# Six damage items of an attention step made by a GpSimd negation and an accumulating DMA, ten kept on VectorE

## The chip, the core and the metric

The kernel runs on one core of a Trainium2 chip. The metric is the device time of one launch in microseconds, the median of several runs. Engines are named as in the profile: PE is TensorE, DVE is VectorE, ACT is ScalarE, POOL is GpSimd, SP is SyncE, which here only issues DMAs.

## What is computed

One transformer layer over x of shape (8, 1024, 128), fp32: a layer norm, then windowed attention and a routed feed-forward (160 experts, 8 chosen for each token) side by side. The change touches the attention alone. With 16 heads and a window of 64 positions, cut to what matters:

```python
disp_win = _windows(disp, 64)                    # (B, heads, T, 64, 16)
strain = disp_win - disp[:, :, :, None, :]
bond_act = gelu(strain @ W_strain + rel_emb @ W_pos)
bond_logits = (bond_act @ W_bond)[..., 0]
damage_act = gelu(strain @ W_dmg + b_dmg)
damage = sigmoid((damage_act @ W_dmg_out)[..., 0] + b_dmg_out[0])
logits = bond_logits - 10.0 * damage
weights = softmax(where(cmask, logits, -inf))
out = einsum('bntd,bntde->bnte', weights, val_win)
```

The products with W_strain and W_dmg are linear in the displacements, so the kernel projects every token once. What is left for a token and a window position is a difference of two projected values, then the gelu.

## The kernel before

The program has five stages: constants, projections and router, `attend(c, 0)`, the experts, `attend(c, 1)`. The two calls of `attend` cover half of the batch each. One call walks over 8 chunks of 512 tokens, each in two steps, one for each group of 8 heads (`par` 0 and 1): 16 steps for each call, 32 in all. Step s has 16 items, n = 0 to 15. Item n is a tile of 128 partitions (8 heads by 16 channels) by 8 window positions by 512 tokens, 4096 fp32 values in a partition, 2 MB in all. Even n are bond items (`ty` 0), odd n are damage items (`ty` 1). An item goes through three engines:

1. The difference of the shifted window (`s_win[..., d0+1 : ...]`) and the values at the token itself ("here"). On DVE "here" comes from PSUM (`ps_here`, which PE fills at L1181). A bond item without bias on ACT is 8 SCALAR_TENSOR_TENSOR (L1102), which add the position term `rpos` as well; a damage item, and in the second call the bond items 6 and 14 (`BIASED`), is one TENSOR_TENSOR of 4096 (L1097). On POOL (L947) it is one TENSOR_TENSOR of two operands in SBUF. `POOL_ITEMS = (3,)`: the damage items 3, 7, 11 and 15 are POOL's, the twelve others DVE's.
2. ACT: one gelu in place (L1001 damage, L1003 bond; 8 for a biased item, L997).
3. PE: matmuls that sum the channels into `ps_l` (L1198), then `item_done`.

DVE has three item buffers: item n waits until item n - 4 is through PE. POOL has two (`u_pool`): item n waits for item n - 8.

Each engine has its own copy of the order, written out by hand, and takes the items strictly in order with other work in between. ACT: tanh (L1010), copies for the softmax (L1019, items 5 to 8), copies of transposed weights (L1032, items 9 to 15 and 0), exp (L1024, item 12, with two table loads). DVE: logits (L1120), mask, maximum, subtraction (L1131, L1135, L1138, items 8 to 11), the sum, its reciprocal and in the first call the multiply by it (L1142, L1145, L1148, item 15); in the second call also 32 additions of routed rows (L1074), 8 at each of the items 0, 4, 8 and 12. POOL: behind each of the items 3, 7, 11 and 15 `route`, 8 indirect DMAs (L926 scatters rows in the first call, L935 gathers them in the second); at item 3 of every second step `spread` (L913), which waits until PE has finished the value products of the chunk before (`av_done`, the last of them at PE's item 1 of the same step); at item 5 of the same steps an addition (L959); at item 15 of the second call the multiply by the reciprocal (L963), which waits for DVE's L1145.

SP loads the windows (L765), waiting in L757 to L763 until every subtraction that reads the same `s_win` is through, and carries the weights to DRAM and back (L793, L799, 2 MB back for each step).

Of the kernel before, what the change touches and what calls it, by code (L numbers as in the profile page):

```python
# [32 lines left out]
TOPK = 8  # L33
POOL_ITEMS = (3,)
BIASED = (6, 14)


def moe_attention_layer(nc, x, w_dispT, w_val, relT, w_strain, w_pos, w_bond, w_dmg, b_dmg,
# [28 lines left out]
    with ExitStack() as ctx:  # L67
# [3 lines left out]
        def sem(name):  # L71
            return ctx.enter_context(nc.semaphore(name))
# [38 lines left out]
        def sb(name, shape, dt=F32, c=ctx):  # L111
            return c.enter_context(nc.sbuf_tensor(name, shape, dt))
# [542 lines left out]
        win_loaded = [sem(f"win_loaded{g}") for g in range(HG)]  # L655
        sub_dve, sub_pool, gelu_done, item_done = sem("sub_dve"), sem("sub_pool"), sem("gelu_done"), sem("item_done")
        tanh_done, logits_in = sem("tanh_done"), sem("logits_in")
# [15 lines left out]
        def attend(c, half):  # L673
# [7 lines left out]
            chunk0 = (1 - half) * NCH // 2 - it0  # L681
            u_dve = sb(f"u_dve_{half}", [P, 3, 8, TC], F32, c)
            u_pool = sb(f"u_pool_{half}", [P, 2, 8, TC], F32, c)
            s_win = sb(f"s_win_{half}", [P, HG, 2, SW], F32, c)
# [24 lines left out]
            ps_u = c.enter_context(nc.psum_tensor(f"ps_u_{half}", [P, TC], F32))  # L709
            on_pool = POOL_ITEMS  # L710
            NP = len(on_pool)
            dve_of = [sum(q % 4 not in on_pool for q in range(n + 1)) for n in range(NI)]
            pool_of = [n + 1 - dve_of[n] for n in range(NI)]
            ND, NPI = dve_of[-1], pool_of[-1]

# [23 lines left out]

            def item_buffer(n):  # L740

                if n % 4 in on_pool:
                    return u_pool[:, (pool_of[n] - 1) % 2]
                return u_dve[:, (n % 4 - sum(q < n % 4 for q in on_pool))]

            def buffer_free(n):

                if n % 4 in on_pool:
                    return n + 1 - 8 // NP
                return n - 3  # L750

            with nc.Block() as block:
                @block.sync
                def _(sp):
                    def load_windows(b, tc, it, par):

                        if some(it):  # L757
                            if some(ND * (2 * it + par - 1)):
                                sp.wait_ge(sub_dve, ND * (2 * it + par - 1))
                                sp.sem_inc(held, 1)  # L760
                            if some(NPI * (2 * it + par - 1)):
                                sp.wait_ge(sub_pool, NPI * (2 * it + par - 1))
# [134 lines left out]
                def _(pool):  # L897
# [41 lines left out]
                    def step(s, it, par, st):  # L939
                        for n in range(NI):  # L940
                            cgrp, d0, ty = offsets(n)
                            if "i" in st and n % 4 in on_pool:
                                if pool_of[n] == 1:
                                    pool.wait_ge(win_loaded[par], 32 * it + 32)
                                if some(NI * s + buffer_free(n)):
                                    pool.wait_ge(item_done, NI * s + buffer_free(n))
# [27 lines left out]
                def _(act):  # L974
# [7 lines left out]
                    def step(s, it, par, st):  # L982
                        for n in range(NI):
# [3 lines left out]
                            if "i" in st:  # L987
                                if n % 4 in on_pool:
                                    if some(NPI * s + pool_of[n]):
                                        act.wait_ge(sub_pool, NPI * s + pool_of[n])  # L990
                                else:
                                    if some(ND * s + dve_of[n]):
                                        act.wait_ge(sub_dve, ND * s + dve_of[n])
                                u = item_buffer(n)
# [54 lines left out]
                def _(dve):  # L1049
# [28 lines left out]
                    def step(s, it, par, st):  # L1078
                        for n in range(NI):
# [5 lines left out]
                            if sums and "i" not in st:  # L1085
                                for d in range(8):
                                    add_routed(s - first, 1 - par, 2 * n + d)
                            if "i" in st and n % 4 not in on_pool:
                                if dve_of[n] == 1:
                                    dve.wait_ge(win_loaded[par], 32 * it + 32)  # L1090
                                    dve.wait_ge(here_done, s + 1)

                                if some(NI * s + buffer_free(n)):
                                    dve.wait_ge(item_done, NI * s + buffer_free(n))
                                here = ps_here[:, ty, :]
                                if ty or n in biased:
                                    last = dve.tensor_tensor(item_buffer(n), windows(par, ty, d0, 8),  # L1097
                                                             here.unsqueeze(1).to_broadcast([P, 8, TC]), ALU.subtract)
                                else:

                                    for d in range(8):
                                        last = dve.scalar_tensor_tensor(  # L1102
                                            out=item_buffer(n)[:, d, :], in0=s_win[:, par, ty, d0 + d + 1:d0 + d + 1 + TC],
                                            scalar=rpos[:, d0 + d:d0 + d + 1], in1=here, op0=ALU.add, op1=ALU.subtract)
# [49 lines left out]
                def _(pe):  # L1154
# [30 lines left out]
                    def step(s, it, par, st):  # L1185
                        more = "i" in st and (not isinstance(s, int) or s + 1 < end)
                        for n in range(NI):
                            cgrp, d0, ty = offsets(n)
                            if "i" in st:
# [6 lines left out]
                                for d in range(8):  # L1196
                                    q, g = (d0 + d) % 16 // 4, d % 4
                                    last = pe.matmul(ps_l[32 * g:32 * g + 32, cgrp % 2, ty, :], wsel[:, ty, q, :],  # L1198
                                                     item_buffer(n)[:, d, :], start=(q == 0), stop=(q == 3))
                                last.then_inc(item_done, 1)  # L1200
# [264 lines left out]
```

## Time and profile before

| | |
|---|---|
| median of 3 runs | 4021.71 us (4020.48 to 4023.9) |
| the profiled execution | 4033.82 us, span 4032.3 us |
| busy, share of the span | DVE 84%, ACT 64%, PE 63%, POOL 61% |
| first call of attend, from 379 us to 1722 us | DVE 1318.45 us busy of 1342.70 |
| experts, 1722 us to 2371 us | not touched |
| second call, 2371 us to 4032 us | DVE 1540.48 us busy of 1661.00 |

Times are read from one execution. A group's line gives busy time, the mean of one instruction and, behind the bar, the idle time of its engine just before the instructions and what ended it. PE's busy time is pipelined, so it says little of its limit.

### The profile page before, as it was taken

Reading aid. Unit: us, or ns where it says so; the run is one execution under the profiler, and the core shown is the slowest. Engines: PE = TensorE matmul, PEld = TensorE weight load, DVE = VectorE, ACT = ScalarE, POOL = GpSimd, SP = SyncE. Lnnn points to the kernel's source line nnn. Section 1 sums busy time; section 2 is a strip of 40 time slices with the busy share of each in tenths; the row PEclk is TensorE's granted clock in tenths of the full one; section 3 lists DMA queues with packets and bytes.
Section 4 is the critical chain, followed back from the end, with each engine's and each line's share of the span. In section 5 each row is a group of like instructions: output and inputs, shape, how many; then the busy total and the mean of one; then the engine's idle time right before and its main releaser. Section 6 shows DMA issues by size and latency. Waiting matters only on the chain. (4 is left out here: it accounts for less than half of the span.)

```text
span 4032.3 us, 64337 instructions
## 1 busy us (share of the span) xinstructions
PE 2547.4 (63%) x20970; PEld 1282.8 (32%) x20970; DVE 3379.6 (84%) x4350; ACT 2576.9 (64%) x1812; POOL 2476.6 (61%) x1748
## 2 busy tenths in 40 slices
PE   5661556766666666668888864565666656565556
PEld 3440112322222222246667631122222222222224
DVE  6886999999999999923433369999999999999993
ACT  1111878888788887833333356777777777777773
POOL 1222887668787787813333467677767767676762
PEclk9885878888888888879999987777878787878886
DMA  7883121322222222127887841222222222222222
GB/s 258 304 304 99 37 74 63 96 81 78 72 70 84 91 80 75 58 79 235 243 243 240 244 139 32 68 65 74 64 75 64 75 64 75 64 75 64 74 63 81
DMA packets 376227, 445.81 MB, mean 111 GB/s; under 512 B 49185, under 2 KB 291697, under 8 KB 376050
## 3 DMA queue, kind: packets, MB, share of 16 engines
q1 hardware_dynamic: 293106, 283.77, 22.4%
q0 software_dynamic: 58752, 148.46, 11.3%
q10 hardware_dynamic: 24192, 11.02, 1.0%
q8 instruction: 134, 2.20, 0.2%
q14 instruction: 43, 0.35, 0.0%
HBM read 239.08 MB, written 204.02 MB: 110 GB/s over the span
## 5 line engine op out<-in xcount | busy, mean ns | idle before, releaser
L1198 PE MATMUL ps_l<-u_dve,wsel 128*32 128x512 f32 x6144 | 1004.0, 780 | 1001.8 <-ACT u_dve L1003 640.7
L1102 DVE SCALAR_TENSOR_TENSOR u_dve<-s_win,rpos,ps_here 128x512 f32<-128x512 f32 x1792 | 1225.8, 737 | 74.3 <-PE ps_here L1181 51.4
L1003 ACT ACTIVATE u_dve<-u_dve 128x4096 f32<-128x4096 f32 x224 | 809.9, 3616 | 427.8 <-DVE u_dve L1102 427.0
L947 POOL TENSOR_TENSOR u_pool<-s_win 128x4096 f32<-128x4096 f32 x128 | 1021.9, 7983 | 9.7 <-PE ps_l L1198 6.9
L1097 DVE TENSOR_TENSOR u_dve<-s_win,ps_here 128x4096 f32<-128x4096 f32 x160 | 703.0, 4409 | 0.0
L1198 PEld LDWEIGHTS ps_l<-u_dve,wsel 128*32 128x32 f32 x6144 | 211.1, 128 | 1447.7 <-issue 647.1
L926 POOL DMA_INDIRECT xslot_dram<-xr,slot_now x512 | 520.0, 1016 | 154.1 <-issue 147.8
L935 POOL DMA_INDIRECT yg<-yslot_dram,slot_now x512 | 499.1, 975 | 164.6 <-issue 144.1
L1001 ACT ACTIVATE u_dve<-u_dve,bdmg_sb 128x4096 f32<-128x4096 f32 x128 | 474.6, 3708 | 91.5 <-DVE u_dve L1097 86.8
L1001 ACT ACTIVATE u_pool<-u_pool,bdmg_sb 128x4096 f32<-128x4096 f32 x128 | 473.7, 3701 | 27.7 <-POOL u_pool L947 27.5
L1391 DVE TENSOR_TENSOR hs<-sg,ps_e 128x512 f32<-128x512 f32 x168 | 115.4, 687 | 382.6 <-ACT sg L1376 382.6
L1074 DVE SCALAR_TENSOR_TENSOR acc<-yg,gate_now,acc 128x128 f32<-128x128 f32 x512 | 358.9, 701 | 1.0
L1198 PE MATMUL ps_l<-u_pool,wsel 128*32 128x512 f32 x2048 | 267.2, 636 | 113.9 <-ACT u_pool L1001 113.3
L1168 PE MATMUL ps_o<-at_sb,v_msk 128*32 128x64 f32 x4096 | 303.7, 235 | 0.1
L1168 PEld LDWEIGHTS ps_o<-at_sb,v_msk 128*32 128x32 f32 x4096 | 268.7, 120 | 75.0 <-issue 56.0
L1369 ACT ACTIVATE xsT<-ps_x 128x512 f32<-128x512 f32 x168 | 100.3, 597 | 277.8 <-PE ps_x L1329 277.8
L1032 ACT ACTIVATE at_sb<-ps_u 128x512 f32<-128x512 f32 x256 | 150.8, 589 | 190.9 <-PE ps_o L1168 162.1
L963 POOL TENSOR_TENSOR ml<-ml,winv 128x2048 f32<-128x2048 f32 x16 | 72.6, 4537 | 320.2 <-DVE slot_now L1058 184.2
L1407 POOL DMA_DIRECT2D yslot_dram<-ys x168 | 128.1, 762 | 216.4 <-DVE ys L1397 189.3
L1246 PEld LDWEIGHTS ps_u<-ident,band 128*128 128x128 f32 x1024 | 148.2, 198 | 297.3 <-issue 183.5
L1246 PE MATMUL ps_u<-ident,band 128*128 128x128 f32 x1024 | 203.7, 329 | 58.1 <-ACT at_sb L1032 39.4
L1138 DVE TENSOR_TENSOR ml<-ml,mx 128x512 f32<-128x512 f32 x128 | 205.4, 1604 | 4.4
(142 smaller groups left out, 3366.2 us busy)
## 6 DMA issues: line engine op xcount, KB each, us to landing
band<-band_dram SPq DMA_DIRECT2D x32, 2048.0 KB
xslot_dram<-zero SPq DMA_DIRECT2D x16, 2688.0 KB, 10.1
xs<-xslot_dram SPq DMA_DIRECT2D x168, 256.0 KB, 3.6
yslot_dram<-ys POOLq DMA_DIRECT2D x168, 256.0 KB, 3.2
band_dram<-ml SPq DMA_DIRECT2D x64, 512.0 KB
we<-in_w_expert SPq DMA_DIRECT2D x336, 64.0 KB, 2.8
s_win<-s_dram SPq DMA_DIRECT2D x64, 288.0 KB, 8.2
s_dram<-s_sb POOLq DMA_DIRECT2D x16, 1024.0 KB, 4.6
```

What stands on the lines that cost most here:

```text
L926: pool.indirect_dma_start(xslot_dram, bass.IndirectOffsetOnAxis(ap=slot_now[:, par, i:i + 1], axis=0), xr[:, par, j, :], None).then_inc(sc ...
L935: pool.indirect_dma_start(yg[:, i, :], None, yslot_dram, bass.IndirectOffsetOnAxis(ap=slot_now[:, par, i:i + 1], axis=0)).then_inc(gathere ...
L947: pool.tensor_tensor(item_buffer(n), windows(par, ty, d0, 8), s_win[:, par, ty, PAD:PAD + TC].unsqueeze(1).to_broadcast([P, 8, TC]), ALU.s ...
L1001: act.activation(u, u, ACT.Gelu, bias=bdmg_sb[:]).then_inc(gelu_done, 1)
L1003: act.activation(u, u, ACT.Gelu).then_inc(gelu_done, 1)
L1074: dve.scalar_tensor_tensor(out=acc[:, old, j, :], in0=yg[:, i, :], scalar=gate_now[:, old, i:i + 1], in1=acc[:, old, j, :], op0=ALU.mult, ...
L1097: last = dve.tensor_tensor(item_buffer(n), windows(par, ty, d0, 8), here.unsqueeze(1).to_broadcast([P, 8, TC]), ALU.subtract)
L1102: last = dve.scalar_tensor_tensor(out=item_buffer(n)[:, d, :], in0=s_win[:, par, ty, d0 + d + 1:d0 + d + 1 + TC], scalar=rpos[:, d0 + d:d0 ...
L1138: dve.tensor_tensor(ml[:, j], ml[:, j], mx[:, j, :].unsqueeze(1).to_broadcast([P, D, HH]), ALU.subtract).then_inc(centred, 1)
L1168: last = pe.matmul(ps_o[32 * g:32 * g + 32, j * P + half * HALF:j * P + (half + 1) * HALF], v_msk[:, 2 * j + half, 32 * h:32 * h + 32], at ...
L1198: last = pe.matmul(ps_l[32 * g:32 * g + 32, cgrp % 2, ty, :], wsel[:, ty, q, :], item_buffer(n)[:, d, :], start=(q == 0), stop=(q == 3))
L1246: last = pe.transpose(ps_u[:, i * P:(i + 1) * P], band[:, k // 2, 4 * (k % 2) + i:BANDW:HH], ident[:])
```

## The change

Six damage items of a step, 3, 5, 7, 11, 13 and 15, are made in two parts. POOL writes the negated "here" values, broadcast over the 8 positions, into the item's buffer with one TENSOR_SCALAR (multiply by -1), waits for its own semaphore, and issues an accumulating DMA that adds the 8 shifted windows from `s_win` onto that buffer, SBUF to SBUF. ACT waits for the DMA's semaphore (one for each buffer) in place of POOL's. The damage items 1 and 9 and all bond items are DVE's, ten in all. The numbers of buffers stay 3 and 2, but both sets now rotate over the items of their own kind: a DMA item waits for the second last DMA item before it, a DVE item for the third last DVE item. SP's load of the windows waits for `gelu_done` of the earlier step's items in place of the two subtraction semaphores. The cut diff:

```diff
-POOL_ITEMS = (3,)
+DMA_ITEMS = (3, 5, 7, 11, 13, 15)
+DVE_BUFS = 3
+DMA_BUFS = 2
...
+            def slot_of(m):
+                par, n = m // NI % 2, m % NI
+                if n in DMA_ITEMS:
+                    return "dma", (par * NM + DMA_ITEMS.index(n)) % DMA_BUFS
+                return "dve", (par * ND + on_dve.index(n)) % DVE_BUFS
...
+            def buffer_free(par, n):
+                m = par * NI + n
+                back = next(k for k in range(1, 2 * NI + 1) if slot_of(m - k) == slot_of(m))
+                return n - back + 1
...
-                            if some(ND * (2 * it + par - 1)):
-                                sp.wait_ge(sub_dve, ND * (2 * it + par - 1))
...
+                            if some(NI * (2 * it + par - 1)):
+                                sp.wait_ge(gelu_done, NI * (2 * it + par - 1))
...
-                                pool.tensor_tensor(
-                                    item_buffer(n), windows(par, ty, d0, 8),
-                                    s_win[:, par, ty, PAD:PAD + TC].unsqueeze(1).to_broadcast([P, 8, TC]),
-                                    ALU.subtract).then_inc(sub_pool, 1)
+                                u = item_buffer(par, n)
+                                pool.tensor_scalar(
+                                    u, s_win[:, par, ty, PAD:PAD + TC].unsqueeze(1).to_broadcast([P, 8, TC]),
+                                    -1.0, None, ALU.mult).then_inc(base_set, 1)
+                                pool.wait_ge(base_set, NM * s + k + 1)
+                                pool.sem_inc(held, 1)
+                                pool.dma_start(u, windows(par, ty, d0, 8), accum_op=ALU.add)\
+                                    .then_inc(sub_dma[landed(it, par, n)[0]], 16)
...
-                                if n % 4 in on_pool:
-                                    if some(NPI * s + pool_of[n]):
-                                        act.wait_ge(sub_pool, NPI * s + pool_of[n])
+                                if n in DMA_ITEMS:
+                                    i, count = landed(it, par, n)
+                                    act.wait_ge(sub_dma[i], count)
...
-                            if "i" in st and n % 4 not in on_pool:
+                            if "i" in st and n not in DMA_ITEMS:
```

## Rows read from the trace of the kernel before

**Rows 1.** Windows over 11 steps of each call: busy us (x instructions), granted clock, DMA
```profile
core 0: us, PE busy (x) PEld busy (x) DVE busy (x) ACT busy (x) POOL busy (x), PEclk, DMA share, GB/s
706.40:1644.50 938.10, 619.84 (x4860) 261.11 (x4852) 923.66 (x936) 782.78 (x398) 719.38 (x445) 0.88 0.25 79
2746.00:3844.00 1098.00, 665.62 (x4852) 267.14 (x4848) 1064.18 (x1123) 816.05 (x563) 766.42 (x461) 0.80 0.23 70
```
**Rows 2.** Groups of DVE in the first call's window, 706.4:1644.5
```profile
L1102 DVE SCALAR_TENSOR_TENSOR u_dve<-s_win,rpos,ps_here 128x512 f32<-128x512 f32 x704 | 468.8, 737 | 11.8 <-PE ps_here L1181 11.8
L1097 DVE TENSOR_TENSOR u_dve<-s_win,ps_here 128x4096 f32<-128x4096 f32 x44 | 194.0, 4410 | 0.0
...
L1142 DVE TENSOR_REDUCE wsum<-ml 128x32 f32<-128x2048 f32 x11 | 42.7, 3879 | 0.0
```
**Rows 3.** Groups of ACT and POOL in the first call's window
```profile
L1003 ACT ACTIVATE u_dve<-u_dve 128x4096 f32<-128x4096 f32 x89 | 321.8, 3616 | 81.5 <-DVE u_dve L1102 81.1
...
L1001 ACT ACTIVATE u_pool<-u_pool,bdmg_sb 128x4096 f32<-128x4096 f32 x44 | 162.9, 3702 | 23.2 <-POOL u_pool L947 23.2
L1032 ACT ACTIVATE at_sb<-ps_u 128x512 f32<-128x512 f32 x88 | 51.8, 589 | 41.6 <-PE ps_o L1168 41.5
...
L1024 ACT ACTIVATE ml<-ml 128x2048 f32<-128x2048 f32 x11 | 21.0, 1911 | 0.1
L1024 ACT ACT_TABLE_LOAD x11 | 14.1, 1283 | 0.2
...
L926 POOL DMA_INDIRECT xslot_dram<-xr,slot_now x348 | 358.1, 1029 | 99.9 <-issue 99.9
L947 POOL TENSOR_TENSOR u_pool<-s_win 128x4096 f32<-128x4096 f32 x43 | 343.2, 7981 | 0.8
L913 POOL COPY v_msk<-v_raw 128x128 f32<-128x128 f32 x48 | 11.6, 293 | 123.6 <-PE ps_o L1168 104.1 <-issue 19.5
```
**Rows 4.** Group of POOL in the second call's window, 2746:3844
```profile
L963 POOL TENSOR_TENSOR ml<-ml,winv 128x2048 f32<-128x2048 f32 x11 | 49.9, 4540 | 221.4 <-DVE slot_now L1058 120.8 <-DVE winv L1145 100.6
```
**Rows 5.** Groups of POOL over the whole span
```profile
L1407 POOL DMA_DIRECT2D yslot_dram<-ys x168 | 128.1, 762 | 216.4 <-DVE ys L1397 189.3 <-issue 27.0
L1306 POOL DMA_DIRECT2D we<-in_w_expert x168 | 90.1, 536 | 121.4 <-issue 67.7 <-PE ps_z L1355 53.1 <-DVE ys L1397 0.7
...
L898 POOL MEMSET v_msk<- 128x4096 f32 x2 | 7.0, 3508 | 73.4 <-POOLq L620 68.8 <-POOLq L1278 4.7
```
**Rows 6.** Timeline of one hand-over from ACT to PE, first call
```profile
902.75 3.61 ACT L1003 ACTIVATE u_dve<-u_dve 128x4096 f32<-128x4096 f32 x1
...
906.41 1.92 PE L1198 MATMUL ps_l<-u_dve,wsel 128*32 128x512 f32 x16 [0.50 <-ACT u_dve L1003]
```
**Rows 7.** DMA issues: KB each, us to landing
```profile
s_dram<-s_sb POOLq DMA_DIRECT2D x16, 1024.0 KB, 4.6
...
band_dram<-zero SPq DMA_DIRECT2D x1, 4096.0 KB, 12.4
```
**Rows 8.** DVE lines with two operands in SBUF: ns min/median/max, whole span
```profile
L1074 DVE SCALAR_TENSOR_TENSOR acc<-yg,gate_now,acc x512: 258/339/8114, 2444.0 to 3970.5; 128x128 f32<-128x128 f32 x171
L1138 DVE TENSOR_TENSOR ml<-ml,mx x128: 691/693/8456, 488.9 to 3967.2; 128x512 f32<-128x512 f32 x128
```
**Rows 9.** Timeline: one DVE addition, then a POOL subtraction and a DVE subtraction beside it
```profile
3116.75 7.80 DVE L1074 SCALAR_TENSOR_TENSOR acc<-yg,gate_now,acc 128x128 f32<-128x128 f32 x1
...
929.20 8.20 POOL L947 TENSOR_TENSOR u_pool<-s_win 128x4096 f32<-128x4096 f32 x1
...
933.40 4.55 DVE L1138 TENSOR_TENSOR ml<-ml,mx 128x512 f32<-128x512 f32 x1
```
**Rows 10.** Waits of SP, the window loads' own
```profile
SPq L760 <- DVE u_dve L1102: 60.9, 1, 60.9
SPq L760 <- DVE u_dve L1097: 59.9, 1, 59.9
```

More of the change, by code:

```diff
@@ L655, in moe_attention_layer @@
         win_loaded = [sem(f"win_loaded{g}") for g in range(HG)]
-        sub_dve, sub_pool, gelu_done, item_done = sem("sub_dve"), sem("sub_pool"), sem("gelu_done"), sem("item_done")
+        sub_dve, gelu_done, item_done = sem("sub_dve"), sem("gelu_done"), sem("item_done")
+        base_set, sub_dma = sem("base_set"), [sem(f"sub_dma{i}") for i in range(DMA_BUFS)]
         tanh_done, logits_in = sem("tanh_done"), sem("logits_in")
@@ L681, in attend @@
             chunk0 = (1 - half) * NCH // 2 - it0
-            u_dve = sb(f"u_dve_{half}", [P, 3, 8, TC], F32, c)
-            u_pool = sb(f"u_pool_{half}", [P, 2, 8, TC], F32, c)
+            u_dve = sb(f"u_dve_{half}", [P, DVE_BUFS, 8, TC], F32, c)
+            u_dma = sb(f"u_dma_{half}", [P, DMA_BUFS, 8, TC], F32, c)
             s_win = sb(f"s_win_{half}", [P, HG, 2, SW], F32, c)
@@ L709, in attend @@
             ps_u = c.enter_context(nc.psum_tensor(f"ps_u_{half}", [P, TC], F32))
[L710 to L714, printed above, removed]
+            on_dve = [n for n in range(NI) if n not in DMA_ITEMS]
+            dve_of = [sum(q in on_dve for q in range(n + 1)) for n in range(NI)]
+            ND, NM = len(on_dve), len(DMA_ITEMS)
+            def slot_of(m):
[3 more added lines that the diff above has]
+                return "dve", (par * ND + on_dve.index(n)) % DVE_BUFS
             def steps(e, step):
@@ L738, in windows, with item_buffer, landed @@
                 return bass.AP(row.tensor, row.offset, [list(row.ap[0]), [1, nd], [1, TC]])
-            def item_buffer(n):
-                if n % 4 in on_pool:
[L743 to L750, printed above, removed]
+            def item_buffer(par, n):
+                which, i = slot_of(par * NI + n)
+                return (u_dma if which == "dma" else u_dve)[:, i]
+            def buffer_free(par, n):
+                m = par * NI + n
+                back = next(k for k in range(1, 2 * NI + 1) if slot_of(m - k) == slot_of(m))
+                return n - back + 1
+            def landed(it, par, n):
+                i = slot_of(par * NI + n)[1]
+                uses = [m for m in range(2 * NI) if slot_of(m) == ("dma", i)]
+                return i, 16 * (len(uses) * it + sum(m <= par * NI + n for m in uses))
             with nc.Block() as block:
@@ L987, in step @@
                             if "i" in st:
[L988 to L994 removed]
+                                if n in DMA_ITEMS:
+                                    i, count = landed(it, par, n)
+                                    act.wait_ge(sub_dma[i], count)
+                                else:
+                                    act.wait_ge(sub_dve, ND * s + dve_of[n])
+                                u = item_buffer(par, n)
                                 if n in biased:
@@ L1091, in step @@
                                     dve.wait_ge(here_done, s + 1)
-                                if some(NI * s + buffer_free(n)):
-                                    dve.wait_ge(item_done, NI * s + buffer_free(n))
+                                if some(NI * s + buffer_free(par, n)):
+                                    dve.wait_ge(item_done, NI * s + buffer_free(par, n))
                                 here = ps_here[:, ty, :]
                                 if ty or n in biased:
-                                    last = dve.tensor_tensor(item_buffer(n), windows(par, ty, d0, 8),
+                                    last = dve.tensor_tensor(item_buffer(par, n), windows(par, ty, d0, 8),
                                                              here.unsqueeze(1).to_broadcast([P, 8, TC]), ALU.subtract)
@@ L1102, in step @@
                                         last = dve.scalar_tensor_tensor(
-                                            out=item_buffer(n)[:, d, :], in0=s_win[:, par, ty, d0 + d + 1:d0 + d + 1 + TC],
+                                            out=item_buffer(par, n)[:, d, :], in0=s_win[:, par, ty, d0 + d + 1:d0 + d + 1 + TC],
                                             scalar=rpos[:, d0 + d:d0 + d + 1], in1=here, op0=ALU.add, op1=ALU.subtract)
@@ L1198, in step @@
                                     last = pe.matmul(ps_l[32 * g:32 * g + 32, cgrp % 2, ty, :], wsel[:, ty, q, :],
-                                                     item_buffer(n)[:, d, :], start=(q == 0), stop=(q == 3))
+                                                     item_buffer(par, n)[:, d, :], start=(q == 0), stop=(q == 3))
                                 last.then_inc(item_done, 1)
```

13 lines of the change are left out of this document (6 added, 7 removed).

## The prediction

> **What bounds the kernel now.** I read the windows first. Over 11 steps of the first call DVE is busy 923.7 of 938.1 us, that is 84.0 of 85.3 us a step; ACT 71.2 and POOL 65.4. Over 11 steps of the second call a step is 99.8 us, with DVE at 96.7, ACT at 74.2, POOL at 69.7 [rows 1]. The groups of DVE come next: its large ones wait for nobody but 11.8 us for PE [rows 2], while ACT waits for DVE (81.1 us before the bond gelus) [rows 3]. So DVE sets the pace in both calls. DMA is busy 25% and 23% [rows 1]. POOL looks idle a quarter of the time, but its busy time leaves out the issue gaps: 8 scatters a group cost (358.1 + 99.9) / 348 = 1.32 us each, 10 us after each of four items, 40 us a step [rows 3]. POOL really has 32 us of subtractions and 42 us of other work in an 85 us step.
>
> **What leaves.** DVE loses items 5 and 13 and keeps 1 and 9: two TENSOR_TENSOR of 4.41 us, 8.8 us a step [rows 2]. POOL loses four subtractions of 7.98 us, 31.9 us [rows 3]. If DVE stayed the bound, that would be 32 x 8.8 = 282 us.
>
> **A POOL item.** The trace has no one-operand POOL instruction of this size. A memset of the same 4096 columns takes 3.51 us and reads nothing; the two-operand subtraction takes 7.98 [rows 5, 3]. Those are the bounds; I take 4.0, near the memset, since only one operand is added. The issue: 64 KB take 0.54 us and 256 KB 0.76 [rows 5]; for 1024 rows of 2 KB I take 1.1, between 0.8 and 2. With 0.2 for its own semaphore an item costs POOL 5.3 us, six cost 32: nothing is saved there. The Trainium skill (GPSIMD Engine Reference, Engine selection) calls one-input work on GpSimd roughly line-rate; 4096 columns at the 1.2 GHz of its specifications are 3.4 us by that, an estimate, and every POOL item would be 0.6 us cheaper.
>
> **The transfer**, the largest unknown. Copies of 1024 and 4096 KB land after 4.6 and 12.4 us [rows 7]: 2.6 us a MB and 2.0 fixed. The accumulating one writes 2 MB but has two 2 MB inputs, windows and negation. Lower bound: the second input is free, 5.2 us of data. Upper: two reads and a write in series, 15.6. I take the two reads in series with the write beside them, 10.4. Six of these are 62 us a step beside the 20 that are there, out of 85, so they meet: with half of the present 25% share falling into them, 10.4 becomes 12. It then lands 12 + 2.0 - 1.1 = 13 us after its issue ends, and a second one behind it no sooner than 12 us after the first. The rule "the accumulate reads its destination and writes it later" (the Trainium skill, DMA: Bandwidth & Descriptors, Rules for kernel authors) speaks against the change in the same direction; no row here shows such a transfer.
>
> **The loop.** A DMA item goes round: negate and issue 5.3, land 13, gelu 3.7 [rows 3], PE 2.8 (it ends 2.0 us after the gelu in [rows 6], more at the lower clock). POOL waits for the buffer with all its queue behind it: item 7 for 3, 11 for 5, 13 for 7, 15 for 11, 3 for 13, 5 for 15. Due times in the first call, zero when item 3's issue ends; 15 of the step before was issued at -15.3 (a route group of 10 and item 3 lie between). Step with no `spread`: 3 is through ACT at 17.3 and PE at 20.1; POOL issues 5 at 15.3 and 7 at 25.4; they land at 28.3 and 40.3; 5 is through PE at 34.8; 7 leaves ACT at 44.0; 11 is issued at 40.7, but ACT has 8 to 11 and small copies, 17.1 us, so 11 leaves ACT at 61.1 and PE at 63.9; 15 is issued at 69.2; a route group, and item 3 of the next step (13 is through PE at 76.4) at **84.5**. Step with `spread`: PE's item 1 and the values are done at 13.1, copies to 15.1, so 5 is issued at 30.4, 7 at 37.0; they land at 43.4 and 55.4; 11 leaves ACT at 76.2; 15 at 84.3; next item 3 at **99.6**. `spread` costs POOL 17 us a time now as well (104.1 us before six groups of 8 copies [rows 3]), hidden because a POOL item has 8 items' time to come round; that cover goes. A pair takes 184.1 against 170.6 now: +13.5 x 8 = +108.
>
> Second call: after 15, POOL's multiply waits for DVE's reciprocal, and the route group and item 3 queue behind it. 11 leaves ACT at 61.1, 12 at 64.8, exp with its tables (1.9 + 2 x 1.28 [rows 3]) 69.3, DVE's sum 3.9 [rows 2] and reciprocal 73.6, multiply 4.5 [rows 4], route, item 3: **93.5**. With `spread`, 4 us of wait and 2.4 of copies, everything 6.4 later: **99.9**. A pair 193.4 against 199.6: -6.2 x 8 = -50. POOL's 20 us wait a step for the reciprocal (221.4 us in 11 [rows 4]) is about what the loop uses up.
>
> **At no cost.** The window load waits for a later event, but is needed a step on; SP waited for it only at the start, 60.9 and 59.9 us [rows 10]; cover gone, it would cost up to a step. Scatters and gathers queue behind the accumulates by up to 12 us, and are read a step later. DVE's three rotating buffers only reach further ahead. Contention: a DVE line with two SBUF operands stretches beside a POOL subtraction: 339 ns at the median and 8114 at most, 693 and 8456 [rows 8], and one took 4.55 us until the POOL instruction ended [rows 9]. The Trainium skill (SBUF — State Buffer, Who interferes with whom) says that such a DVE instruction contends with any GpSimd instruction that reads SBUF. By that the negation blocks too, 24 us a step against 32. It matters only if DVE binds; I count it at nothing.
>
> **Sum.** 4033.8 + 108 - 50 = 4092 for the profiled execution, which stands 12.1 above the median of the runs: **4080 us**, 1.4% slower. One us more or less on the transfer's data is felt twice a step, at the landings of 5 then 7 and at 11 or the sum: 2 x 32 = 64 us. Clean 10.4 us of data gives 4080 - 1.6 x 64 = 3978; the whole 25% share in the way, 13.9, gives 4202. That is this case's own range.
>
> **Rivals.** About 0.2%, 8 us, is what a measurement of this kernel can tell from no change.
>
> Rival 1, faster: the second input is nearly free and the transfer lands in 6 to 8 us. Then DVE's saving comes through until ACT or POOL binds: the first call's step cannot go under POOL's 74 plus part of `spread`, say 78, the second under DVE's 96.7 - 8.8 = 88. That gives 16 x (7.3 + 11.8) = 306 less, 3720 at best; 3800 if half the waits stay. For: copies of 4 MB run at 2.6 us a MB with 25% load. Against: two inputs. Chance 0.18.
>
> Rival 2, DMA becomes the bound: 15.6 us of data, six and the 20 now there are 114 us a step. Both calls then run at 114: 16 x (28.7 + 14.2) = +686, 4710. It decides from where the six pass 65 us in the first call. For: nothing in the trace shows the adder's rate. Chance 0.12.
>
> Rival 3, POOL's own work: negation at 6 us and issue at 2 make an item 8.2, three of them lie on the path of a step, +2.9 x 3 x 32 = +278, 4360. Chance 0.10.
>
> My forecast's case has 0.60: of it 0.20 ends faster by over 0.2%, where the interference is small, 0.07 within, 0.33 slower. Together: faster 0.38, same 0.07, slower 0.55. Range 3820 to 4300: it takes the own range, most of rival 1 and the near part of 3, and leaves out about 0.1 on either side.
>
> **What would show it.** The duration of the POOL TENSOR_SCALAR (4.0), the accumulate's issue (1.1) and landing (14 from its start); ACT's wait before damage gelus passing from POOL and DVE to a DMA; POOL's waits for PE before the negations; DVE's busy share falling to about 0.85 in the first call with waits for PE. Right steps would show 84 and 100 us in turn in the first call. Wrong it is if a landing takes under 10 us, if DVE still runs at 98%, or if DMA is busy over 95%.

## The result and the profile after

| | before | changed |
|---|---|---|
| median of 4 runs | 4021.43 us | 5278.18 us (5270.16 to 5282.32) |
| span of the profiled execution | 4032.3 us | 5280.8 us |
| DVE, ACT, POOL busy, share of the span | 84%, 64%, 61% | 69%, 49%, 72% |

The changed kernel is slower by a factor of 1.313 (95% interval 1.311 to 1.315), 1257 us. The forecast was 4080 us, 59 slower, with a range from 3820 to 4300: the direction was right, the size was not, by a factor of twenty. The first view is the table of windows over the same 11 steps of each call as in [rows 1]; the columns are those of [rows 1].

```profile
core 0: us, PE busy (x) PEld busy (x) DVE busy (x) ACT busy (x) POOL busy (x), PEclk, DMA share, GB/s
851.50:2300.10 1448.60, 674.03 (x4844) 276.98 (x4844) 878.77 (x914) 781.88 (x397) 1183.05 (x538) 0.73 0.73 147
3577.00:5050.50 1473.50, 703.94 (x4844) 276.17 (x4844) 1290.71 (x1101) 817.95 (x562) 1234.80 (x550) 0.73 0.74 147
```

A step of the first call went from 85.3 to 131.7 us, one of the second from 99.8 to 134.0. Times 16 each that is 742 and 547, together a little over the whole loss, since the first steps of each call lost less. DVE no longer sets the pace in the first call: 79.9 us busy a step. POOL is busy 107.5. PE's granted clock read 0.88 before and reads 0.73 now in the first call, where PE is busy 47% of the time in place of 66%.

Next, the groups of POOL in the first of these windows; [rows 3] has their counterparts.

```profile
L963 POOL TENSOR_SCALAR u_dma<-s_win 128x4096 f32<-128x4096 f32 x66 | 710.5, 10766 | 12.2 <-PE ps_l L1216 10.8
L939 POOL DMA_INDIRECT xslot_dram<-xr,slot_now x352 | 354.1, 1006 | 106.3 <-issue 105.7 <-PE ps_l L1216 0.6
L968 POOL DMA_DIRECT2D u_dma<-s_win x66 | 111.0, 1681 | 47.1 <-POOL u_dma L963 28.4 <-issue 12.1 <-DVE slot_now L1076 6.6
...
L926 POOL COPY v_msk<-v_raw 128x128 f32<-128x128 f32 x48 | 11.6, 287 | 99.9 <-PE ps_o L1186 87.2 <-issue 12.7
```

The one-operand multiply takes 10.77 us, more than the two-operand subtraction that it replaces (7.98 [rows 3]). The issue takes 1.68. With the wait between them (28.4 + 12.1 + 6.6 over 66) an item holds POOL for 13.2 us, six hold it for 79, the routing for 42 more: 121 of the 131.7 us. Nearly all of the rest is the value copies and the stand before them, (99.9 + 11.6) / 11 = 10.1 us. POOL waits for an item's buffer 10.8 us in 11 steps. The buffer loop, on which the forecast's due times rest, is not where the time goes: POOL reaches each item so late that its buffer has long been free. The timeline of POOL shows one stand (start, duration, instruction, idle before it):

```profile
1131.36 1.71 POOL L968 DMA_DIRECT2D u_dma<-s_win  x1 [0.61 <-POOL u_dma L963]
1151.30 1.94 POOL L926 COPY v_msk<-v_raw 128x128 f32<-128x128 f32 x8 [18.24 <-PE ps_o L1186]
```

The steps of the first call alternate accordingly, mostly 122 and 142 us. POOL's waits in the second call's window (us in total, times, longest) show the same queue there:

```profile
POOL yg L948 <- issue: 104.0, 348, 0.3
POOL u_dma L968 <- POOL u_dma L963: 44.9, 65, 1.0
POOL ml L982 <- DVE winv L1163: 37.2, 3, 13.6
POOL v_msk L926 <- PE ps_o L1186: 31.9, 3, 10.9
POOL ml L982 <- DVE slot_now L1076: 13.6, 1, 13.6
```

A step has 112.3 us of POOL's busy time and 13.5 of gaps at its own issues; it stands 4.6 for DVE's reciprocal and 2.9 before the value copies. That is 133.3 of 134.0 us: POOL's queue fills the step in both calls.

Two views answer to the transfer: the issues by line (KB each, us to landing), and the DMA queue of POOL (packets, MB, share of 16 engines), 11.3% before.

```profile
u_dma<-s_win POOLq DMA_DIRECT2D x192, 2048.0 KB, 15.1
...
q0 software_dynamic: 258432, 551.13, 54.0%
```

If the rest of this queue costs what it did before (456 us; it is 456 and 460 in two later runs without the transfers), 192 transfers took 0.540 x 5280.8 - 0.113 x 4032.3 = 2396 us of all 16 engines, 12.5 us each. A transfer lands 15.1 us after its start at the median and 14.1 at the least.

### The profile page after: what moved, and what is told of

It reads as the page before. It is cut to its first block and busy times, and to the rows that moved or that the text cites. A ratio compares the mean times of both kernels' runs of the same rounds, so it can differ in the third digit from the quotient of the medians.

```text
span 5280.8 us, 64909 instructions
## 1 busy us (share of the span) xinstructions
PE 2683.3 (51%) x20970; PEld 1305.1 (25%) x20970; DVE 3630.5 (69%) x4286; ACT 2580.1 (49%) x1812; POOL 3814.6 (72%) x2004
## 5 line engine op out<-in xcount | busy, mean ns | idle before, releaser
L963 POOL TENSOR_SCALAR u_dma<-s_win 128x4096 f32<-128x4096 f32 x192 | 2068.8, 10775 | 25.3 <-PE ps_l L1216 20.9
L1216 PE MATMUL ps_l<-u_dma,wsel 128*32 128x512 f32 x3072 | 647.7, 988 | 1605.1 <-ACT u_dma L1019 1605.1
L1019 ACT ACTIVATE u_dma<-u_dma,bdmg_sb 128x4096 f32<-128x4096 f32 x192 | 711.8, 3707 | 1359.7 <-DMA u_dma<-s_win 1359.6
L1216 PE MATMUL ps_l<-u_dve,wsel 128*32 128x512 f32 x5120 | 757.5, 708 | 614.4 <-ACT u_dve L1021 410.9
L1092 DVE SCALAR_TENSOR_TENSOR acc<-yg,gate_now,acc 128x128 f32<-128x128 f32 x512 | 677.2, 1323 | 1.9 <-DMA acc<-part_dram 0.9
L1216 PEld LDWEIGHTS ps_l<-u_dma,wsel 128*32 128x32 f32 x3072 | 113.0, 152 | 1917.5 <-ACT u_dma L1019 1389.2
L1115 DVE TENSOR_TENSOR u_dve<-s_win,ps_here 128x4096 f32<-128x4096 f32 x96 | 423.4, 4410 | 0.0
L968 POOL DMA_DIRECT2D u_dma<-s_win x192 | 322.6, 1680 | 133.7 <-POOL u_dma L963 105.4
L1156 DVE TENSOR_TENSOR ml<-ml,mx 128x512 f32<-128x512 f32 x128 | 341.4, 2667 | 4.4
L1186 PEld LDWEIGHTS ps_o<-at_sb,v_msk 128*32 128x32 f32 x4096 | 271.6, 121 | 79.9 <-issue 61.7
L1019 ACT ACTIVATE u_dve<-u_dve,bdmg_sb 128x4096 f32<-128x4096 f32 x64 | 237.0, 3703 | 45.6 <-DVE u_dve L1115 45.6
## 6 DMA issues: line engine op xcount, KB each, us to landing
u_dma<-s_win POOLq DMA_DIRECT2D x192, 2048.0 KB, 15.1
```

Of the source, the lines that this page charges most:

```text
L963: pool.tensor_scalar(u, s_win[:, par, ty, PAD:PAD + TC].unsqueeze(1).to_broadcast([P, 8, TC]), -1.0, None, ALU.mult).then_inc(base_set, 1)
L968: pool.dma_start(u, windows(par, ty, d0, 8), accum_op=ALU.add)\
L1092: dve.scalar_tensor_tensor(out=acc[:, old, j, :], in0=yg[:, i, :], scalar=gate_now[:, old, i:i + 1], in1=acc[:, old, j, :], op0=ALU.mult, ...
L1115: last = dve.tensor_tensor(item_buffer(par, n), windows(par, ty, d0, 8), here.unsqueeze(1).to_broadcast([P, 8, TC]), ALU.subtract)
L1156: dve.tensor_tensor(ml[:, j], ml[:, j], mx[:, j, :].unsqueeze(1).to_broadcast([P, D, HH]), ALU.subtract).then_inc(centred, 1)
L1186: last = pe.matmul(ps_o[32 * g:32 * g + 32, j * P + half * HALF:j * P + (half + 1) * HALF], v_msk[:, 2 * j + half, 32 * h:32 * h + 32], at ...
```

## The experiments

The theory after this reading: POOL's queue is the bound, and the multiply overfills it. The rivals: the transfers bound it, a hidden wait of the loop, or contention between POOL and DVE. Where no ratio is given, a kernel has one time; the kernel before beside them stood between 4011 and 4028 us.

### The multiply, replaced in three ways

```diff
-                                pool.tensor_scalar(
-                                    u, s_win[:, par, ty, PAD:PAD + TC].unsqueeze(1).to_broadcast([P, 8, TC]),
-                                    -1.0, None, ALU.mult).then_inc(base_set, 1)
+                                pool.memset(u, 0.0).then_inc(base_set, 1)
```

> The negation is replaced by a memset of the same 4096 columns, so the damage items leave out the token's own value. Theory (POOL's queue is the bound, and the negation of 10.6 us is what overfills it): the memset takes 3.5 us, a POOL item 6.1 us, POOL's work of a step falls from 120 to 78 us, and the buffer loop of the prediction decides: with 15 us landings about 88 us a step without the value copies and 103 with them, 4200 us in all. Rival (the accumulating transfer itself is the bound, with DMA 73% busy): the time stays above 4700 us and DMA's busy share rises over 0.9.

```diff
+                                pool.tensor_copy(
+                                    u, s_win[:, par, ty, PAD:PAD + TC].unsqueeze(1).to_broadcast([P, 8, TC]))\
+                                    .then_inc(base_set, 1)
```

> The negation is replaced by a copy of the same broadcast row (the minus sign is left out). Theory A (any one-operand POOL instruction over 4096 columns with a broadcast input is slow): the copy takes about 10 us and the time stays at 5280 us. Theory B (the multiply by a constant is slow, the pattern is not): the copy takes 4 to 5 us and the time falls to 4250 us or so.

```diff
+                                pool.tensor_tensor(
+                                    u, zero[:, 0:TC].unsqueeze(1).to_broadcast([P, 8, TC]),
+                                    s_win[:, par, ty, PAD:PAD + TC].unsqueeze(1).to_broadcast([P, 8, TC]),
+                                    ALU.subtract).then_inc(base_set, 1)
```

> The negation is written as a two-operand subtraction, a broadcast row of zeros minus the broadcast row; the result is the same as the changed kernel's. Theory (the one-operand form is dearer than the two-operand one): the subtraction takes 8.2 us as in the kernel before, a POOL item 10.8 us, a step 106 us and with the value copies 126: about 4800 us. Rival (writing beside an accumulating transfer slows any POOL instruction, so the subtraction stretches too): it takes over 10 us and the time stays near 5280.

Measured: 4338 us with the memset, 4345 with the copy, 5067 with zeros minus the row. The groups of POOL and DVE over the whole span, the memset first:

```profile
L963 POOL MEMSET u_dma<- 128x4096 f32 x192 | 682.6, 3555 | 366.0 <-PE ps_l L1214 362.7 <-issue 2.5 <-DMA s_win<-s_dram 0.6
...
L1090 DVE SCALAR_TENSOR_TENSOR acc<-yg,gate_now,acc 128x128 f32<-128x128 f32 x512 | 180.8, 353 | 12.4 <-issue 11.4
```

the copy:

```profile
L963 POOL COPY u_dma<-s_win 128x4096 f32<-128x4096 f32 x192 | 701.0, 3651 | 357.8 <-PE ps_l L1216 353.6 <-issue 3.2 <-DMA s_win<-s_dram 0.5
...
L1092 DVE SCALAR_TENSOR_TENSOR acc<-yg,gate_now,acc 128x128 f32<-128x128 f32 x512 | 388.9, 759 | 9.0 <-issue 8.0
```

and the subtraction from zeros:

```profile
L963 POOL TENSOR_TENSOR u_dma<-zero,s_win 128x4096 f32<-128x4096 f32 x192 | 1732.7, 9024 | 31.2 <-PE ps_l L1217 27.9 <-DMA s_win<-s_dram 0.8
```

The same broadcast row is copied in 3.65 us and multiplied in 10.77. So the multiply is dear and the pattern is not: theory B of the copy's expectation. With seven us less an item, 933 us are gone (940 with the memset), and only now POOL waits for the buffers, 354 us. The rival of the memset run fell in its number (it wanted over 4700) but not in its mark: DMA's share rose to 0.94 in the first call. The time was 140 above my 4200. The zeros-minus form was expected at 8.2 us and 4800 us; it took 9.0 and 5067, between the theory and the rival (over 10 us, near 5280). The steps of its first call fell to 113 and 132 us in turn, those of its second only to 129 from 134, which the expectation had not seen. Why this subtraction takes 9.0 and not the 8.0 of the kernel before is open.

A finding beside it: DVE's additions with two SBUF operands take 353 ns at the mean with the memset, which only writes, 759 with the copy, which reads for 3.65 us, and 1323 in the changed kernel, where the multiply reads for 10.77. The last beside that of the kernel before:

```profile
L1074 DVE SCALAR_TENSOR_TENSOR acc<-yg,gate_now,acc 128x128 f32<-128x128 f32 x512 | 358.9, 701 | 1.0
...
L1092 DVE SCALAR_TENSOR_TENSOR acc<-yg,gate_now,acc 128x128 f32<-128x128 f32 x512 | 677.2, 1323 | 1.9 <-DMA acc<-part_dram 0.9
```

That the time hardly differs between memset and copy, 4338 and 4345, also says that this contention does not bound these two kernels. The three means agree with the Trainium skill (SBUF — State Buffer, Who interferes with whom), which sets writing apart from reading.

### The value copies at item 7

```diff
-                            if "a" in st and n == 3 and par == 0:
+                            if "a" in st and n == 7 and par == 0:
                                 spread(it - 1)
```

> The value copies of POOL (spread) move from item 3 to item 7 in its order, nothing else. Theory: in every second step POOL stands 18 us at item 3 for PE's value products, with the whole queue behind it; at item 7 they are long done, so every second step falls from 142 to about 124 us: 15 x 18 = 270 us less, about 5010 us. Rival (the wait only moves to another place, as POOL would otherwise wait for item buffers): under 100 us less.

Measured 5180 us, 98 less, against 270 expected: inside the rival's mark of under 100. The stand is gone, and the long steps of the first call fell from 142 to 127 us. The expectation took 18 us for all 15 copies; the changed kernel's whole wait there is 119.1 us for PE and 33.4 without a named releaser, 152 us, most of it in the first call.

### The negated row made elsewhere

The same result without the long multiply: ACT writes one negated row of 512 columns a step, POOL copies it over the positions; the value copies at item 7.

```diff
+                    def negate(s, it, par):
+                        if some(NM * s):
+                            act.wait_ge(base_set, NM * s)
+                        act.wait_ge(win_loaded[par], 32 * it + 32)
+                        act.activation(negrow[:], s_win[:, par, 1, PAD:PAD + TC], ACT.Copy, scale=-1.0).then_inc(neg_set, 1)
...
+                                pool.tensor_copy(
+                                    u, negrow[:].unsqueeze(1).to_broadcast([P, 8, TC])).then_inc(base_set, 1)
```

> ACT writes one negated row of 512 for the damage items once a step (0.6 us), POOL copies it over the 8 positions (3.6 us in place of 10.6), and the value copies stand at item 7: the same result with POOL's item at 6.2 us and no 18 us stand. Theory (with POOL relieved the two-buffer loop of the prediction is the bound, and half of what the value copies' wait cost comes off): 4345 us of the run with the copy alone, less about 8 x 18 in the first call and some 50 in the second: 4150 us, still slower than before. Rival (the loop's other waits refill it): 4300 or more.

Measured 4310 us: the rival. DMA was 94% busy in both calls. The same edit with four items, and the value copies back at item 3:

```diff
-DMA_ITEMS = (3, 5, 7, 11, 13, 15)
+DMA_ITEMS = (3, 7, 11, 15)
```

> The same negated row and copy, but only the four items 3, 7, 11 and 15 go through the accumulating DMA, as POOL's four did before; DVE has its twelve items again. POOL's item costs 6.2 us in place of 8.2, and of these only 3.6 us read SBUF beside DVE, so DVE's lines with two SBUF operands are held up for 14 us a step in place of 32. Theory (contention is worth half of DVE's 11 us of stretching): both calls 5 us a step shorter than in the kernel before, 3860 us. Rival (the longer way of an item, 27 us against 8, makes ACT wait): 4030 to 4150.

Measured 4079 us, a ratio of 1.016 (1.014 to 1.019), against 3860 expected: the rival again. POOL waited 246 us for ACT's row, a wait that the experiment itself brought in.

### Half a transfer, and four items with the multiply

The first edit stands on the kernel with the copy.

```diff
-                                pool.dma_start(u, windows(par, ty, d0, 8), accum_op=ALU.add)\
+                                pool.dma_start(u[:, 0:4], windows(par, ty, d0, 4), accum_op=ALU.add)\
```

> As the run with the copy, but the DMA adds only four of the eight windows (the other four are left out), so its data are 1 MB. Theory of the loop: 5.6 us less at each landing, felt twice a step, 32 x 11 = 358 us less than 4345, about 3990. Rival (POOL's queue of 78 us and the value copies are the bound, transfers are hidden): less than 100 us less.

Measured 3967 us, 379 below the run with the whole transfer. Once the multiply is gone, the transfer is on the path, 11.8 us a step for about half of its data. The number is near the expected 358, but not for the expectation's reason: DMA fell from 93% to 66% busy in the first call, and POOL's queue is what fills its steps of 88.1 us now, with 78.3 us of work and 8.2 of standing before the value copies; it waits for item buffers 1.4.

> The changed kernel with its own negation on POOL but only the items 3, 7, 11 and 15 by DMA. Theory (POOL's queue is the sum of its items at 13.2 us and 41 us of routing): 94 us a step, 112 with the value copies' wait, second call 94 to 110: about 4420 us. Rival (with six items DMA itself was the trouble, four are fine): under 4200.

The edit is that of the four items, on the changed kernel. Measured 4588 us, above both expectations. Its POOL group is 10.60 us an item, and the sum for POOL is right, 94 us and more. But the steps of the first call took 97 to 117 and those of the second 109 and 123 in turn. Over 11 steps of the first call, 106.4 us each, POOL's work is 95.3; the rest is the stand before the value copies, 7.9, and before the addition that waits for ACT, 3.1. In the second call, 116.8 us a step, POOL has 100.7 of work, 10.8 of waiting for DVE's reciprocal and 5.9 for ACT. So POOL's queue with its waits for others fills the step in both calls; the expectation had taken too little of the waits.

### Nobody waits for a row, four items

POOL negates one row of 512 columns itself once a step and copies it; the value copies at item 7, or at item 3.

```diff
+                                row = zero[:, par * TC:(par + 1) * TC]
+                                if k == 0:
+                                    pool.tensor_scalar(row, s_win[:, par, ty, PAD:PAD + TC], -1.0, None, ALU.mult)\
+                                        .then_inc(neg_set, 1)
+                                    pool.wait_ge(neg_set, s + 1)
+                                    pool.sem_inc(held, 1)
+                                pool.tensor_copy(u, row.unsqueeze(1).to_broadcast([P, 8, TC])).then_inc(base_set, 1)
```

> Four DMA items (3, 7, 11, 15); POOL negates one row of 512 columns itself once a step (1.4 us if the multiply costs 2.6 ns a column whatever its pattern) and copies it over the positions at each item, and the value copies stand at item 7. POOL then waits neither for ACT's row (246 us in the run with four items) nor 18 us for PE. Theory (with POOL on time the loop has slack, DVE is the bound with less contention): 83 us a step in the first call, 95 in the second, about 3900 us. Rival (POOL's lateness was harmless and the 15 us landing itself makes ACT late): 4040 to 4080 as before.

> As the run beside it, but the value copies stay at item 3. Theory: every second step of the first call stands up to 15 us on POOL, of which four items' distance hides part: 50 us more than the run beside it. Rival (hidden as in the kernel before): no difference.

Measured 3979 us (ratio 0.990, 0.989 to 0.992) and 3985 us (0.992, 0.991 to 0.994): both are faster than the kernel before, by one per cent and not the three expected, and by far faster than the changed one. The groups of POOL in the first of the two:

```profile
L969 POOL COPY u_dma<-zero 128x4096 f32<-128x4096 f32 x128 | 467.9, 3656 | 8.2 <-POOL zero L965 5.4 <-PE ps_l L1220 2.4
...
L965 POOL TENSOR_SCALAR zero<-s_win 128x512 f32<-128x512 f32 x32 | 49.1, 1534 | 24.5 <-PE ps_l L1220 16.2 <-issue 6.9 <-DMA s_win<-s_dram 0.7
```

512 columns, with no broadcast, cost 1.53 us, 3.0 ns a column; 4096 with a broadcast cost 2.6 a column. That is the second sign that the operation is slow whatever the pattern. In the eleven middle steps of each call this kernel stands at 85.8 and 99.6 us, as before. What it gains lies in the first four steps of each call, 309 us against 327 in the first and 353 against 375 in the second. DVE's additions fell from 701 to 505 ns, and in the first call DVE is busy only 79.0 us a step in place of 84.0. But it waits there for ACT's copies and exp (48 us in 11 steps) and for "here" from PE (19), and in the second call for item buffers on PE (82 us in 11 steps), waits that the kernel before has hardly or not at all. So most of what contention gave back went into waits; that the longer way of an item brings them is likely and not shown. The place of the value copies made no difference with four items.

### Without the transfer, and what bounds six items

```diff
-                                pool.wait_ge(base_set, NM * s + k + 1)
-                                pool.sem_inc(held, 1)
-                                pool.dma_start(u, windows(par, ty, d0, 8), accum_op=ALU.add)\
-                                    .then_inc(sub_dma[landed(it, par, n)[0]], 16)
...
-                                    i, count = landed(it, par, n)
-                                    act.wait_ge(sub_dma[i], count)
+                                    act.wait_ge(base_set, NM * s + DMA_ITEMS.index(n) + 1)
```

> The changed kernel without the accumulating DMA: ACT takes the negated value as it is, so the six items leave out the windows. Theory (POOL's queue alone sets the changed kernel's time): an item costs 10.9 us in place of 13.2, 14 us a step, 440 us less: 4840 us. Rival (the transfers carry a good part of the 1257 us): under 4600.

The other run is the edit of the section before (POOL's row, value copies at item 7) with all six items.

> Six DMA items as in the change, with POOL's own negated row once a step, the copies, and the value copies at item 7. Theory (with POOL at 80 us a step the transfers bound it: DMA was 94% busy in the run with ACT's row): 4250 to 4310, no better than that run's 4310. Rival (waiting for ACT's row cost it): 4150 or less.

Measured 4753 us without the transfer and 4318 for six items with POOL's row. The first is 526 below the changed kernel where POOL's shorter item alone explained 440, and still 737 above the kernel before, with no transfer in it at all: the multiply is enough to lose by. The multiply itself takes 10.59 us there, so the transfers beside it are not what makes it slow. Here are its windows:

```profile
780.00:1948.40 1168.40, 654.53 (x4844) 267.58 (x4844) 982.87 (x915) 783.41 (x398) 1065.50 (x473) 0.79 0.20 64
3162.90:4536.50 1373.60, 663.23 (x4844) 265.71 (x4844) 1282.72 (x1101) 815.12 (x563) 1121.80 (x483) 0.74 0.19 56
```

The first call's step is 106.2 us, POOL's sum of six times 10.6 and 42. The second call's is 124.9, with DVE busy 93% of it, its additions at 1410 ns each over the run. POOL works 111 us of that step and stands 11.3 for DVE's reciprocal. In the second call the multiply costs twice, on POOL and through the longer instructions of DVE that POOL then waits for.

The windows of the six items with POOL's row:

```profile
740.50:1832.50 1092.00, 639.66 (x4844) 267.15 (x4844) 744.57 (x914) 779.39 (x398) 741.70 (x550) 0.81 0.96 195
2964.20:4120.60 1156.40, 671.29 (x4844) 270.27 (x4844) 933.27 (x1101) 815.42 (x562) 784.07 (x560) 0.78 0.92 186
```

DMA is 96% busy in the first call, at 99.3 us a step; the second call has 105.1.

The last two runs take up what was open: why six items with the copy stand at 4318 and not at the forecast's 4080.

```diff
-DVE_BUFS = 3
-DMA_BUFS = 2
+DVE_BUFS = 2
+DMA_BUFS = 3
```

> As the six-item run with POOL's own row and late value copies (4318 us), but three buffers for the DMA items and two for DVE's. Theory A (DMA is saturated at 6 x 11.2 + 20 = 87 us of every step and more with bursts): 4250 to 4350, no real change. Theory B (two buffers are the bound, a third takes the wait for PE before POOL's copies away): 4100 or less. DVE's two buffers could cost something on either theory.

The edit stands on the six items with POOL's row. Measured 4290 us. The waits of POOL's copies for an item's buffer, with two buffers:

```profile
POOL u_dma L969 <- PE ps_l L1220: 285.0, 58, 11.4
```

and with three:

```profile
POOL u_dma L969 <- PE ps_l L1220: 3.9, 4, 2.0
```

The wait vanished and the time stayed. But a new wait came in its place, for DVE now has only two buffers. DVE's waits for its own, with three buffers and with two:

```profile
DVE u_dve L1124 <- PE ps_l L1220: 51.2, 10, 9.3
...
DVE u_dve L1124 <- PE ps_l L1220: 415.5, 103, 14.9
```

The windows of this run show what is left:

```profile
721.10:1800.00 1078.90, 656.50 (x4848) 269.16 (x4844) 797.85 (x914) 782.75 (x399) 737.82 (x549) 0.79 0.97 196
2914.70:4097.90 1183.20, 665.93 (x4844) 266.61 (x4844) 892.04 (x1101) 815.90 (x563) 782.14 (x560) 0.80 0.91 182
```

DMA is 97% busy in the first call, where no engine is busy over 75%. Theory A, saturation, holds for the first call. The second call went from 105.1 to 107.6 us a step with DMA at 91%: there DVE's new wait may hide what the third buffer gave, and what holds the second call 8 to 10 us a step above its DMA work stays open.

> As the six-item run with POOL's own row and late value copies, without the accumulating DMA (the six items leave out the windows). It gives what ten DVE items are worth when both the multiply and the transfer are gone. Theory (DVE 75 us, ACT 72 us a step in the first call, DVE 86 in the second): 78 and 88 us a step, 3730 us. Rival (POOL's 66 us with its waits still binds, or contention does): 3900 or more.

This is the run of 4318 us without its transfers. Measured 3770 us, near the 3730 expected. Its windows:

```profile
674.70:1510.00 835.30, 582.79 (x4852) 254.51 (x4848) 759.36 (x915) 776.82 (x399) 642.18 (x481) 0.92 0.28 89
2566.90:3591.40 1024.50, 644.17 (x4844) 267.74 (x4844) 931.61 (x1101) 814.65 (x563) 673.15 (x494) 0.83 0.25 76
```

75.9 and 93.1 us a step, where 78 and 88 were expected: this is what ten DVE items are worth, 241 us below the kernel before beside it, if the other six cost no transfer and no long multiply. ACT is then at 93% in the first call. DVE's busy time fell from 84.0 to 69.0 us a step there and from 96.7 to 84.7 in the second call, by more than the 8.8 us of two items. In the first call the rest is in its lines with two SBUF operands, which stand beside shorter reads of POOL now: `ml<-ml,winv` went from 5099 to 2292 ns at the mean, `ml<-ml,mx` from 1684 to 1097, `ml<-ml,mask_t` from 1718 to 700.

The 1257 us split along these runs: from the kernel before to this floor -241; the transfers +548 (3770 to 4318); the multiply in place of row and copy, and the value copies' place, +960 (4318 to 5278); the kernel before stood 10 us lower beside the floor run than beside the changed kernel, which is the difference to 1257. Taken in the other order, the parts are nearly the same: the multiply and the copies' place +982 without transfers (3770 to 4753), the transfers +526 with the multiply.

## Why the prediction was wrong

**What bounds the kernel, and what leaves DVE:** right. DVE set the pace, and 8.8 us a step left it. That 241 of the 282 us come out when nothing takes their place is in part luck: DVE's busy time fell by 14.9 and 12.0 us a step, as its lines with two SBUF operands became shorter too, and the step followed only by 9.3 and 6.7.

**"I take 4.0, near the memset, since only one operand is added":** this step failed, and it decides. The multiply took 10.77 us, 6.8 more, and lay even above the upper bound of 7.98 that I had set. A two-operand instruction is no upper bound for a one-operand one of another kind. The bounds were set by the number of operands, but the cost went with the operation: a copy of the same row, which also has one operand, is at 3.65, near what I took. In the prediction's sum of POOL's queue, six items at 5.3 us were 32; they are six at 13.2, 79, and with the 42 of routing 121 us of work in a step that had been 85. The Trainium skill's line on one-input work (GPSIMD Engine Reference, Engine selection), by estimate 3.4 us at the clock that the page gives, holds for the copy (3.65) and not for the multiply by a constant (10.77). Rival 3 had the nearest mechanism, POOL's own work, but priced the negation at 6 us, counted three items on the path of a step where all six and the routing stand in one queue, and gave it 0.10.

**The issue at 1.1 us:** 1.68, inside the bounds given.

**The transfer, "two reads in series with the write beside them, 10.4":** the size was nearly right. Each took 12.5 us of all engines where the sum, with its load, had 12; that is 2.4 times the 5.2 of a plain copy. It landed 15.1 after its start, where the sum had 14.1. That the two reads stand in series is not shown. Nor is the load shown to stretch a transfer: by the same sum it took 12.3 us in the runs with DMA over 90% busy, and 12.5 with 73%.

**"so they meet: with half of the present 25% share falling into them, 10.4 becomes 12":** the second step that failed. Six at 12.5 are 75 us and the 20 beside them make 95: a step cannot be shorter than that, and with POOL's row the six-item runs stood at 98 to 99 in the first call. The own rule of rival 2, "from where the six pass 65 us", was met, and already by the forecast's own 12 us, six of which are 72. I had kept the queue as a stretch of one transfer and not as a sum over a step. In the first call that is what puts the cheap negation near 4310 in place of 4080; the second call's part of it stays open.

**The loop's due times:** not tested in the changed kernel, where POOL is later than any buffer. With the copy the loop's waits appear (354 us on POOL), the steps of the first call alternate between 92 and 113 us (due times 84.5 and 99.6), and halving the rows took off about 2 us a step for each us of data. That looks like the loop as written, and is luck: with half the rows POOL hardly waits for buffers. In the first call, where DMA is 96% busy with two buffers and 97% with three, the buffer waits are the form that a full DMA takes and not the cause. For the second call the third buffer does not settle it.

**`spread`'s cover goes:** right. It cost 18 us in every second step of the first call, and 98 us in all.

**Contention "at nothing":** wrong for the second call. With a 10.8 us read six times a step, DVE's additions went from 701 to 1323 ns, and DVE, with two items fewer, was busy 117.3 us a step in place of 96.7. POOL stood 4.6 us a step for DVE's reciprocal in the changed kernel, and 11.3 without transfers, where DVE was 93% busy.

**DVE's three buffers "only reach further ahead":** not quite. DVE waited 114 us for item buffers in the changed kernel and never before; it was not the engine that set the pace.

**What was to show it:** of the signs named, the first, the duration of the TENSOR_SCALAR against 4.0, was the one that told. "DMA busy over 95%" became true only once the multiply was gone, and in the first call alone.

## What to carry to other kernels

Price an engine's instruction by a row of the same operation; a row with more operands is no upper bound for another operation, and where no such row exists, measure that one instruction before anything is built on it. For a queue that many parts share, sum its time over a whole period first, DMA included, and only then work out a loop through it. When a large part goes to another engine, a broadcast row can be prepared once and copied, as the multiply of 512 columns and four copies did here, for one per cent.

## What the runs showed of the hardware

On POOL a multiply by a constant over 4096 fp32 columns takes 10.6 to 10.8 us, a copy 3.6 to 3.8, a memset 3.5 to 3.6, a subtraction of two SBUF operands 7.98 to 9.0. 512 columns of the multiply without a broadcast take 1.53. An accumulating DMA of 2 MB from SBUF to SBUF takes 12.3 to 12.5 us of all 16 engines, 1.7 us of POOL to issue, and lands 15 to 16 us after its start at the median. DVE's additions of 128 columns with two SBUF operands take 353 ns at the mean beside memsets of POOL, 759 beside its copies and 1323 beside its multiplies.
